# Expert weights held in two places of on-chip memory instead of four, in a mixture-of-experts layer on one core

## The reference

```
logits = x2d @ gate_kernel                  # 2048 rows, 32 experts
weights, chosen = top_k(softmax(logits), 8) # 8 experts for each row
rows sorted by expert, group_sizes = rows of each expert
w0 = ragged_dot(sorted, gate_proj)          # 512 -> 192
w1 = ragged_dot(sorted, up_proj)            # 512 -> 192
out = ragged_dot(silu(w0) * w1, down_proj)  # 192 -> 512
output = sum over the 8 experts of weight * out
```

## Time and profile before

| | us |
|---|---|
| median of three runs | 1531.71 |
| lowest and highest | 1529.96, 1535.05 |
| the profiled execution | 1529.96 |
| its span, first to last instruction | 1528.0 |
| PE busy | 1414.2 (93%) |
| DVE busy | 1018.2 (67%) |
| ACT busy | 507.9 (33%) |
| POOL busy | 385.2 (25%) |
| mean granted clock of PE | 0.967 of full |

### The profile page before, as it was taken

The page is one execution under the profiler, slowest core; times in us unless marked ns, Lnnn a source line. Parts: engine busy times, 40 slices in busy tenths (PEclk is TensorE's granted clock), DMA queues, the critical chain, the costliest instruction groups (busy, mean ns, idle before and its releaser), DMA issues.

```text
span 1528.0 us, 27230 instructions
## 1 busy us (share of the span) xinstructions
PE 1414.2 (93%) x7616; PEld 768.2 (50%) x7617; DVE 1018.2 (67%) x2461; ACT 507.9 (33%) x922; POOL 385.2 (25%) x314
## 2 busy tenths in 40 slices
PE   5699999999999999988989729999999999999997
PEld 3344444444444444444444315666666666666664
DVE  6859856964884546576776645666666666666665
ACT  1335444443344343332122103333333333323332
POOL 1000000000000000014546452344343444344443
PEclk9789999999999999999999959999999999999999
DMA  9946676765676578727665767889999899989787
GB/s 375 410 157 213 231 251 213 250 222 183 203 239 216 194 258 286 262 64 276 224 216 202 288 235 182 220 217 248 247 254 236 224 233 230 251 224 214 157 151 128
DMA packets 133845, 347.01 MB, mean 227 GB/s; under 512 B 15136, under 2 KB 19744, under 8 KB 126880
## 3 DMA queue, kind: packets, MB, share of 16 engines
q1 hardware_dynamic: 74528, 208.56, 40.4%
q0 software_dynamic: 34784, 86.00, 24.5%
q10 hardware_dynamic: 24480, 51.80, 10.7%
HBM read 194.43 MB, written 151.88 MB: 227 GB/s over the span
## 4 chain that ended last, share of the span: by engine, by line
PE 75%; DVE 10%; DMA 5%; issue 4%; another core or an unknown queue 2%; ACT 2%; SPq 1%; ACTq 1%; DVEq 0%; POOLq 0%
PE PS L1400 19%; PE PS L1398 19%; PE PS L1399 19%; PE PS L1626 5%; PE PS L1653 2%; PE PS L1652 2%; DMA split_experts<-HT 2%; PE PS L1641 1%; PE PS L1642 1%; DMA BIG<-in_wdT 1%; DMA CST<-in_kv 1%; PE PS L1361 1%; PE PS L1393 1%; PE PS L1394 1%
## 5 line engine op out<-in xcount | busy, mean ns | idle before, releaser
L557 POOL DMA_INDIRECT out<-BIG,EX x160 | 249.1, 1557 | 362.6 <-issue 155.5
L1398 PE MATMUL PS<-BIG 128*128 x804 | 271.4, 338 | 3.2 <-DVE BIG L1319 1.4
L1399 PE MATMUL PS<-BIG 128*128 x804 | 271.4, 338 | 0.0
L1400 PE MATMUL PS<-BIG 128*128 x804 | 271.4, 338 | 0.0
L1398 PE MATMUL PS<-HT,BIG 128*128 128x512 f16 (+1 forms) x512 | 195.4, 382 | 4.8 <-ACT EX L607 2.9
L1399 PE MATMUL PS<-HT,BIG 128*128 128x512 f16 (+1 forms) x512 | 195.5, 382 | 0.0
L1400 PE MATMUL PS<-HT,BIG 128*128 128x512 f16 (+1 forms) x512 | 195.2, 381 | 0.0
L535 POOL DMA_INDIRECT rows_by_expert<-HT,POS x128 | 124.6, 974 | 142.6 <-DVE POS L1217 107.7
L1398 PE MATMUL PS<-BIG,EX 128*128 128x512 f16 (+1 forms) x384 | 146.3, 381 | 6.9 <-DVE EX L1159 5.0
L1399 PE MATMUL PS<-BIG,EX 128*128 128x512 f16 (+1 forms) x384 | 146.3, 381 | 0.0
L1400 PE MATMUL PS<-BIG,EX 128*128 128x512 f16 (+1 forms) x384 | 146.2, 381 | 0.0
(11 more groups left out here) (224 smaller groups left out, 2258.0 us busy)
## 6 DMA issues: line engine op xcount, KB each, us to landing
BIG<-rows_by_expert ACTq DMA_DIRECT2D x166, 280.0 KB
HT<-in_experts SPq DMA_DIRECT2D x64, 640.0 KB, 4.6
BIG<-split_experts SPq DMA_DIRECT2D x32, 1152.0 KB
split_experts<-HT SPq DMA_DIRECT2D x96, 320.0 KB, 2.3
CST<-in_kv SPq DMA_DIRECT2D x64, 256.0 KB, 4.5
split_context<-RT SPq DMA_DIRECT2D x64, 256.0 KB, 4.4
BIG<-split_context SPq DMA_DIRECT2D x8, 2048.0 KB
rows_by_expert<-X SPq DMA_DIRECT2D x32, 280.0 KB
```

The costliest lines, as they stand in the source:

```text
L557: pool.indirect_dma_start(a_out, bass.IndirectOffsetOnAxis(ap=IDY[:, u % V:u % V + 1], axis=0), yt[u % V], None, compute_op=ALU.add).then_ ...
L1398: mm(out, lh, rh, start=first, stop=False)
L1399: mm(out, lh, rl, start=False, stop=False)
L1400: return mm(out, ll, rh, start=False, stop=last_group)
```

## The change

The number of places for expert weights becomes 2, and the constant `WP` is gone. SP loads two experts before the loop, pads two, and its loop goes over pairs. In the loop the load of expert e waits for the last tile of expert e-2. The place of a tile's expert is its number mod 2. The buffers behind `we` in the same memory (gathered rows, results, split rows, hidden values) move down by 18432 bytes a partition; none changes in size or number.

```diff
-        we = f16(BIG, 0, (WP * E16,))
-        o = WP * E16 // 2
+        we = f16(BIG, 0, (2 * E16,))
+        o = E16
...
-            for e in range(WP):
-                wait(sp, s_wl, 16 * e)
-                load_expert(e, e)
+            load_expert(0, 0)
+            sp.wait_ge(s_wl, 16)
+            load_expert(1, 1)
...
-            for e in range(WP):
-                pad_expert(e, 16 * e)
-            with sp.Fori(1, NE // WP) as i:
-                for h in range(WP):
-                    pad_expert(i * WP + h, i * (16 * WP) + 16 * h)
-                    wait_apart(sp, s_wl, i * (16 * WP) + 16 * h, s_spassed)
-
-                    done = sp.value_load(TCUM[0:1, bass.ds(i * WP + (h - WP), 1)], min_val=1, max_val=NTILE + 1)
+            pad_expert(0, 0)
+            pad_expert(1, 16)
+            with sp.Fori(1, NE // 2) as i:
+                for h in range(2):
+                    pad_expert(i * 2 + h, i * 32 + 16 * h)
+                    wait_apart(sp, s_wl, i * 32 + 16 * h, s_spassed)
+
+                    done = sp.value_load(TCUM[0:1, bass.ds(i * 2 + (h - 2), 1)], min_val=1, max_val=NTILE + 1)
                     sp.wait_ge(s_ed, done)
-                    load_expert(i * WP + h, h)
+                    load_expert(i * 2 + h, h)
...
-            v.tensor_scalar(TAB[:, 2, :], TAB[:, 0, :], WP - 1, None, ALU.bitwise_and).then_inc(s_tq, 1)
+            v.tensor_scalar(TAB[:, 2, :], TAB[:, 0, :], 1, None, ALU.bitwise_and).then_inc(s_tq, 1)
...
-                return load_ints(pe, name, TAB[0:1, 2, bass.ds(t, count)], 0, (WP - 1) * E16)
+                return load_ints(pe, name, TAB[0:1, 2, bass.ds(t, count)], 0, E16)
```

More of the change, by code:

```diff
@@ L44 @@
 SPARES = 4
-WP = 4
 U = 8
```

## The result

| | before | after |
|---|---|---|
| median, us | 1533.38 (4 runs) | 1578.04 (4 runs) |
| lowest and highest | 1529.96, 1535.52 | 1576.26, 1579.22 |
| span of the profiled execution | 1528.0 | 1571.7 |

The ratio is 1.0289, 95% interval 1.0251 to 1.0326: 44 us slower. 1541 was forecast, with a range up to 1557. The direction was right, the size far too small; the second rival (1570.5, with a chance of 0.08) came nearest in its number.

A forecast was written before the change was run, and what follows sets the result against it. PE was taken to bound the experts' stage, with DMA engines busy 0.91. Terms 1.7 + 5.4 + 1.7 + 1.0 + 1.0 = 10.8 us on 1529.96 gave 1540.8, say 1541; range 1535 to 1552, 8 in 10 for 1533 to 1557.

The forecast's parts named there:

- the second rival: Experts' stage: late landings become the rule, loads and gathers sharing busy DMA engines; 40.5 us, 1570.5; chance 0.08.
- How a load's time was read: SP's weight loads: from issue to end of SP's wait, 5.5 to 10.6 us over 27 loads, mean 7.2.
- The deadlines: Experts' stage: a load must land within 5.7 us if 3 tiles cover it, 9.4 for 4, 13.1 for 5.
- (s - 6) x 3.7 + 2.6: Padding's deadline after the load beside it, s being tiles of experts e-2 and e-1 together: 2.6, 6.3, 10.0 us for 6, 7, 8.
- about 0.8 us after the load in front: SP's queue: the padding, issued behind a load, most likely lands then, so 8.0 us after the load's issue.
- Late landings belong to certain places: Weight loads: those after experts 0, 24 and 26 are late against 4 tiles of cover; 1.7 us in all.
- The sum had 1.0 us for this stretch: Around expert 8: load 9 is 0.2 us late, paddings of 9 and 10 are 0.4 late each; together 1.0.
- The clock term: PE's clock falls after the stop at the end of the list: 1.7 us, bounds 0 and 5.
- The end of the list: Experts 29 to 31: padding of 31 lands at 8.0 where 2.6 is needed, 5.4 us; load 31 adds 1.0.
- two places are enough: First rival, experts' stage: loads land in 5.5 to 6.3 us, padding not held up; 2.5 us lost, 1532.5; chance 0.17.
- the volume in flight is unchanged: Argument against late landings as the rule: the transfers' volume stays the same and only its time shifts.
- A faster kernel from two loads fewer in attention: Third rival, attention stage: 3.1 us come back, 1526.9 if the experts' stage loses nothing; chance 0.04.

The follow-up runs named there:

- experiment 14: Changed kernel (two places) with paddings two experts earlier and POOL's adds replaced by a small write: 0.9958 of the kernel before, 1492.82 us.
- experiment 1: Changed kernel (two places) with each padding issued two experts earlier, as with four places: 1.0076 of the kernel before, 11 us slower.
- experiment 5: Changed kernel (two places) with POOL's add of each weighted tile replaced by a small plain write: 1.0015 of the kernel before, 1501.36 us.
- experiment 10: Changed kernel (two places) with rows gathered five tiles ahead instead of six: 1.0091 of the kernel before, 14 us slower.
- experiment 4: Kernel before (four places) with SP waiting for each padding before it waits for the load, to record the landing: 0.9998 of the kernel before.
- experiment 13: Kernel before (four places, early paddings) with ACT kept busy by three extra copies before one silu in eight: 1.0835 of the kernel before, 125 us slower.
- experiment 6: Kernel before (four places) with POOL's add of each weighted tile replaced by a small plain write: 0.9949 of the kernel before, 1492.51 us.
- experiment 2: Kernel before (four places) with each expert's padding issued late, right behind the next expert's load: 1.0238 of the kernel before, 36 us slower.
- experiment 12: Kernel before with SP recording each padding's landing and POOL's adds replaced by a small write; one execution, no time given, paddings landed in 7.2 us on average.
- experiment 3: Changed kernel (two places) with the padding issued ahead of the load instead of behind it: 1.0339 of the kernel before, 51 us slower.
- experiment 7: Three places for expert weights, SP's loop over threes, place e mod 3 computed on the chip: 0.9993 of the kernel before.

## Why the prediction was wrong, by its own steps

**How a load's time was read: right, but for a kernel that does not stop.** 5.5 to 10.6 us and a mean of 7.2 hold in the kernel before and nearly in the one with early paddings (5.6 to 10.8, mean 7.4). In the changed kernel the mean is 8.0, and 19 of 29 take 7.5 us or more.

**The deadlines: right.** 5.7 us for 3 tiles (experiment 14). 9.4 for 4 shows in experiment 1: with loads of 10.2 and 10.1 us against 4 tiles the gaps grew by 0.9 and 0.8, with two of 9.4 and 9.5 by 0.3 each. (s - 6) x 3.7 + 2.6 for the padding shows in experiments 5 and 10. In the changed kernel's first stop the gather left 12.7 us after the load's issue where s = 8 allowed 10.0, and PE stood for 2.76.

**The term that failed is the padding's landing, "about 0.8 us after the load in front".** Measured, it is 2.5 us behind with adds and 1.5 without. My upper bound for it was 2.9 behind the load and 13.5 in all. Four of the 27 pairs of experiment 4 go beyond the 2.9, all behind loads of 6 us or less; the 13.5 held (13.0 there, 13.5 at most in the changed kernel). "The trace never shows it" was wrong as well: nobody waits, but the semaphore's updates are in the trace of before, and by them the paddings landed 9.9 us after the load's issue on average, 13.4 at most (a few updates are missing). The error was to weigh this bound only for s = 6, where every landing is late, and not for s = 8. There are seven pairs of experts with s = 8, their deadline is 10.0, and the bound reached 13.5. With 0.8 they cost nothing and got no line in the sum. With 2.5 the padding of 8, behind a load that took 8.4 in the trace of before (issued at 1035.29, landed at 1043.7), lands at 10.9. Yet this term alone is the smaller part of the miss. With 2.5 in it, and the loads as by place in the trace of before, my sum would have gained 1.7 us for the padding of 31, 1.7 each for those of 9 and 10 and 0.9 for that of 8: by this estimate 17 us instead of 10.8, where 44 were measured.

**"Late landings belong to certain places" failed as well, and cost most.** The places hold only in a kernel that does not stop: in the trace of experiment 4 the loads after experts 4, 17, 24 and 26 again took 9.7 to 10.2 us. Once ACT and PE stop again and again, landings get longer. Behind the loads issued when experts 6 to 12 were done, the padding meets s = 7 or 8 almost each time, so the next stop comes from the longer landing. These loads took 7.7 to 9.9 us in the changed kernel, and those that left at the same ends of experts in the kernel before 5.5 to 6.1. Experiment 13 shows that stops alone bring later landings, experiments 5 and 6 that without the adds no load takes more than 6.5 us, and experiment 2 that two places are not needed for it. That stops and late landings feed each other in the changed kernel is a conclusion from them; it was not shown by itself, and why a stop makes the adds hold up a load more stays open. The sum had 1.0 us for this stretch, where 29 were lost.

**The clock term was sized for one stop.** 1.7 us were set, for the one at the end. In all it was 15.5 over ten stops of PE, 1.6 each: the price was right and the count wrong. Stops of 3.9 us each cost more, 2.6 apiece (experiment 13).

**The end of the list was right in kind.** 8.1 us were set for experts 29 to 31 (5.4 + 1.7 + 1.0). The gap of expert 29 alone grew by 9.4, and load 31 was waited for by 3.3 more. The wait for the padding of 31 is ACT's longest:

```profile
1458.89 0.33 ACT L756 ACTIVATE BIG<-PS 128x192 f32<-128x192 f32 x1 [8.91 <-DMA rows_by_expert<-X]
```

**The rivals.** That two places are enough holds only without add traffic and with early paddings (experiment 14). That late landings become the rule came near in size, but in part by luck: 26.6 of its 40.5 us were waits for weights, while in the run ACT waited 14.0 us for weights and 34.9 for paddings. It has right that landings grew. The reason that I gave against it, "the volume in flight is unchanged", was the wrong thing to look at: in experiment 13 the volume is the same, and the landings are longer. A faster kernel from two loads fewer in attention did not show: the first experts' stage began at the same time within 1.1 us (944.17 against 943.03 for the load after expert 0). The advice to double-buffer (the Trainium skill, Trainium Kernel Development and Optimization, Best Practices) agrees with experiments 1 and 14, where two places cost 11 us and nothing. The change itself cost 44, by what else hung on the same queue.

## What to carry to other kernels

Before you take away buffers, list everything that is issued behind the wait that now comes later, and give each its own deadline: here the small padding, not the large load, made three quarters of the loss. Where an unmeasured duration stands near a deadline that occurs many times, put its upper bound against each of them and add up; a range that weighs it at one place is too narrow. And a stop costs more than its length, by the clock behind it and, where stops keep coming, by later landings; one buffer more (three places), or one tile less of lead, was enough to keep out of it or to take most of it back.

## What the runs showed of the hardware

- A 280 KB write behind a 1152 KB load on one queue landed 1.4 to 4.0 us after the load, 2.5 on average (experiment 4), and 1.5 without POOL's adds (experiment 12). With the order turned the load landed 9.5 us after its issue instead of 7.4 (experiments 3 and 1); how much of that is the padding's and how much comes from the more frequent stops was not separated.
- The same load, with no padding ahead of it, took 5.0 to 6.5 us without POOL's adds (experiments 5, 6 and 14) and 5.4 to 11.3 with them (experiments 7 and 13); the adds' transfers move 256 KB a tile each way.
- A stop of 3.9 us cost 2.6 us more in clock, seen over 20 stops (experiment 13). With four tiles of lead instead of six, loads took 7.9 to 10.3 us with four places and 6.7 to 10.7 with two, and PE waited 70 us for gathered rows with either.
